# Moving GpSimd's wait on the transposes two gathers earlier in a deformable convolution with a following 3x3 convolution

## The reference

```python
x = x + _L0_conv_ref(_gn(x), w_offset, b_offset, w_conv, b_conv, gamma, beta)
x = x + _L1_conv_ref(_gn(x), weight, bias)
```

## Time and profile before

| | |
|---|---|
| median of 3 runs | 948.3 us (947.69 to 948.37) |
| profiled execution, own time | 948.03 us |
| its span, first to last instruction | 946.3 us |
| mean granted TensorE clock | 0.805 |
| gathers, first and last start | 16.1 and 828.6 us |

### The profile page before, as it was taken

One profiled execution on the slowest core, in us unless ns is written; L12 is line 12 of the kernel. 1 busy time (PEld: TensorE's weight loads), 2 busy tenths in 40 slices (PEclk: granted clock), 3 DMA queues, 4 the chain that ended last, 5 costly groups with the idle time before them and its releaser, 6 DMA issues.

```text
span 946.3 us, 8953 instructions
## 1 busy us (share of the span) xinstructions
PE 748.1 (79%) x2436; PEld 351.1 (37%) x2436; DVE 795.8 (84%) x1533; ACT 375.0 (40%) x1026; POOL 669.2 (71%) x731
## 2 busy tenths in 40 slices
PE   7688778877877877787778788778678776879998
PEld 5342322322322322232223323223222222667776
DVE  3789989888889989888899899888889889866664
ACT  3433435434333435433434345343343344453210
POOL 3777777777777777777777777777777777737551
PEclk9876778878768778976887878787797785599999
DMA  7777777777777777777777777777777777711111
GB/s 274 233 200 209 211 210 210 210 209 212 209 211 211 209 212 209 212 209 210 210 210 210 210 212 210 210 212 209 211 209 211 209 210 211 210 33 51 51 51 50
DMA packets 56246, 181.39 MB, mean 192 GB/s; under 512 B 11012, under 2 KB 12036, under 8 KB 55812
## 3 DMA queue, kind: packets, MB, share of 16 engines
q0 software_dynamic: 51840, 169.91, 62.5%
q1 hardware_dynamic: 3924, 10.32, 2.9%
q10 hardware_dynamic: 432, 0.59, 0.2%
HBM read 176.06 MB, written 4.72 MB: 191 GB/s over the span
## 4 chain that ended last, share of the span: by engine, by line
POOL 36%; PE 18%; DVE 18%; issue 14%; DMA 12%; ACT 1%; DVEq 0%; POOLq 0%; ACTq 0%
POOL g L388 36%; DMA g<-corner_table,idx 12%; DVE g L952 7%; PE TP L593 2%; PE PA L593 2%; PE CO L593 2%; PE CO L495 2%; PE TP L507 2%; DVE PA L965 2%; DVE PA L968 2%; DVE acc L971 2%; PE OMT L443 2%; PE VU L593 1%; PE OMT L593 1%; PE PA L438 1%
## 5 line engine op out<-in xcount | busy, mean ns | idle before, releaser
L388 POOL DMA_INDIRECT g<-corner_table,idx x648 | 613.3, 947 | 212.9 <-issue 180.7
L682 ACT ACTIVATE PA<-g,wt 128x128 f32<-128x128 f32 x642 | 203.4, 358 | 459.1 <-DMA g<-corner_table,idx 256.1
L952 DVE TENSOR_TENSOR g<-g,PA 128x1152 f32<-128x1152 f32 (+1 forms) x217 | 291.4, 1343 | 51.5 <-DMA g<-corner_table,idx 50.9
L495 PE MATMUL CO<-cols,wcs 128*128 128x384 f32 (+1 forms) x504 | 260.2, 619 | 78.7 <-ACT cols L663 77.5
L507 PE MATMUL TP<-ident,acc 128*128 128x128 f32 x648 | 146.9, 347 | 101.3 <-DVE acc L971 98.7
L443 PE MATMUL OMT<-xn,woff 128*27 128x384 f32 (+2 forms) x450 | 187.3, 534 | 3.2 <-DVE wt L878 2.0
L495 PEld LDWEIGHTS CO<-cols,wcs 128*128 128x128 f32 x504 | 92.8, 238 | 223.5 <-ACT cols L663 193.7
L507 PEld LDWEIGHTS TP<-ident,acc 128*128 128x128 f32 x648 | 89.1, 171 | 224.9 <-DVE acc L971 211.3
L965 DVE TENSOR_TENSOR PA<-g,PA 128x384 f32<-128x384 f32 x214 | 120.6, 564 | 19.1 <-ACT PA L682 1.2
L968 DVE TENSOR_TENSOR PA<-g,PA 128x384 f32<-128x384 f32 x214 | 119.8, 560 | 5.9
L971 DVE TENSOR_TENSOR acc<-g,PA 128x384 f32<-128x384 f32 x214 | 118.0, 552 | 5.9
(11 more groups left out here) (148 smaller groups left out, 525.9 us busy)
## 6 DMA issues: line engine op xcount, KB each, us to landing
g<-corner_table,idx POOLq DMA_INDIRECT x648, 3.7
out_dram<-x SPq DMA_DIRECT2D x16, 288.0 KB, 2.1
x<-x_dram SPq DMA_DIRECT2D x3, 1152.0 KB, 7.8
x<-x_dram ACTq DMA_DIRECT2D x3, 192.0 KB, 4.2
x<-x_dram SPq DMA_DIRECT2D x3, 192.0 KB, 3.9
wconv<-wconv_dram SPq DMA_DIRECT2D x1, 576.0 KB, 5.0
w<-w_dram SPq DMA_DIRECT2D x1, 576.0 KB, 10.0
grid<-grid_dram SPq DMA_DIRECT2D x1, 162.0 KB, 4.2
```

The costliest lines, as they stand in the source:

```text
L388: pl.indirect_dma_start(out=g[:, k, t].rearrange("p q c -> p (q c)"), out_offset=None, in_=tab_d, in_offset=bass.IndirectOffsetOnAxis(ap=i ...
L495: last = nc.tensor.matmul(co_bank(c, t)[:, t * P:t * P + size], wcs[:, c // CHUNKS % 2, k, :], cols[:, s % TURNS, n * P:n * P + size], sta ...
L682: last = nc.scalar.activation(first[:, n] if s < LAST_SUMS else g[:, k, t, 0, :], g[:, k, t, 0, :], ACT.Copy, scale=wt0[:, c % 2, t, k:k + 1])
L952: nc.vector.tensor_tensor(corners[:, :, 1:4, :], corners[:, :, 1:4, :], weights[:, :, 1:4].unsqueeze(3).to_broadcast([P, size, 3, P]), ALU ...
```

## The change

The wait on `turned` stands inside the loop over an item's gathers: ahead of the second gather of item s (of the only one where an item has one), and it asks that item s + 1 - 4, that is s - 3, is turned. That is the same semaphore value which the kernel before asks for ahead of the first gather of item s + 1, two gathers later. The first gather of an item has no wait on `turned` of its own any more.

```diff
-                    if first_item(c) + i >= LEAD:
-
-                        pl.wait_ge(turned, first_item(c) + i - LEAD + 1)
-                    for k, t in units:
+                    s = first_item(c) + i
+                    for n, (k, t) in enumerate(units):
+                        if n == min(1, len(units) - 1) and s + 1 >= LEAD:
+
+                            pl.wait_ge(turned, s + 1 - LEAD + 1)
                         pl.indirect_dma_start(
```

## The result

Eight runs of the changed kernel have a median of 954.4 us (951.7 to 955.9), eight of the kernel before 948.1 us (945.8 to 949.8). The ratio is 1.0065 with a 95% interval of 1.0050 to 1.0079: slower by 6.2 us (4.7 to 7.5). The forecast was 955.2 us, 6.9 us slower. The profiled execution after has a span of 952.7 us, 6.4 us more than before.

A forecast was written before the change was run, and what follows sets the result against it. The prediction took POOL's gather pace, 1.25 us each with no stall made up, as the bound. Its terms 1.5 + 1.70 + 1.94 + 0.66 + 0.79 + 0.29 = 6.88 us gave 955.2 us, range 951.5 to 960.

The forecast's parts named there:

- POOL's own pace sets the end: From 16 to 829 us gathers start every 1.25 us; no interval makes up for an earlier stall, so delays move the end.
- the first rival: Stalls are absorbed: DVE, the busiest engine, sets the pace and POOL catches up; 948.3 us, chance 5%.
- The price is the lateness of the turns: Cost is how late item s - 3's transposes, plus 0.27 us release, come for item s's second gather; 6.88 us summed.
- The third rival: A release in mid-item is dearer: 0.5 us more at each of seven places, 3.5 in all; 958.7 us, chance 14%.
- start, to item 9: Chunk 0: item 4's second gather waits for item 1 until 36.74, part comes back at 52.98; bounds 1.26 and 2.1, taken 1.5 us.
- chunk 2 (items 18, 19): After the second image's group norm statistics: item 18's gather 0.58 us late, item 19's needs 93.43 against 91.73; 1.70 us in all.
- chunk 8 (item 72): After 2.85 us of DVE statistics at 285.35, item 72's gather at 290.56 needs 292.50: 1.94 us.
- chunk 14 (items 126, 127): Third place after group norm statistics: item 126's gather at 493.21 must wait until 493.87, 0.66 us.
- items 141 to 145: Where DVE computes a group norm's scale; the largest delay is item 145, 564.49 against 565.28: 0.79 us.
- item 177: Its second gather at 684.58 must wait until 684.87: 0.29 us.
- end, item 216: Its wait of 0.58 us costs nothing: the gather lands at 832.81, before DVE reaches the item at 833.83.
- the second rival: Turns come sooner, since part of the lateness is PE's own queue: 4.4 us in all, 952.7 us, chance 18%.

The follow-up runs named there:

- the faster kernel: Kernel before, but the first-gather wait asks for item s - 5 only and, at chunk changes, each gather waits for its own buffer's sum: 0.9976, -2.3 us.
- the control: Kernel before with five of six group norm statistics instructions left out for images 2 to 4: 1.0004 (0.9994 to 1.0014).
- all but the start: Changed kernel with the old wait up to item 8 and the moved wait from item 9 on: 1.0039, +3.7 us against the kernel before.
- before, less statistics: Kernel before with only the first of six group norm statistics instructions kept for images 2 to 4: 1.0004 (0.9994 to 1.0014).
- start alone: Changed kernel with the moved wait for items 3 to 8 only and the old wait from item 9 on: 1.0017, +1.6 us against the kernel before.
- after, less statistics: Changed kernel with five of six group norm statistics instructions left out for images 2 to 4: 1.0019, +1.8 us against the kernel before.
- the other direction: Kernel before with the first-gather wait asking for item s - 5, and per-buffer waits on sums at chunk changes: 0.9976, median 945.8 us.

## Why the prediction was right

**POOL's own pace sets the end.** Shown from three sides: stalls are never made up (no interval between gathers in the changed kernel is under 1.24 us), removing 2.2 us of stalls (2.98 us over the usual idle time before, 0.75 in the faster kernel) gains 2.3 us, and removing 7 us of DVE's work gains nothing. From item 9's third gather to item 215's first, 616 intervals, all six traces whose later waits are no sooner than before take 770.5 to 770.7 us, the one with less work on DVE among them. Nor is this pace that of a backlog of transfers: behind the stall at 31.19 in the changed kernel, where the DMA engines' share from 30 to 32 us was 0.14, the next gather again came 1.25 us later, at 32.44.

Removing DVE's work is the direct test of the first rival. By the Trainium skill (Perfetto Trace Analysis, Identifying the Most-Contended Engine) the engine of highest occupancy is the most contended one and is to be optimized first; that would be DVE, with 84% against POOL's 71%. The trace and the control disagree. What the occupancy leaves out is the idle time of 0.30 us before nearly every one of the 648 gathers, which no wait explains.

**The price is the lateness of the turns.** Shown by the dose: with the same value asked for one, two, three and six gathers sooner the loss is 1.6, 6.2, 29.9 and 370 us, and at the new place with the old value nothing. The third rival, a dearer release, fell: the 15 gathers that the changed kernel's trace holds back start 0.27 us after the transposes, as was taken. The 0.77 us at 52.98, on which it rested, go with the place. In the trace of six gathers sooner the first gather of every chunk but chunk 0 starts 0.77 to 0.80 us after the transposes, and nearly all others 0.27. Ahead of a chunk's first gather other waits stand too; whether they are the reason was not tried.

**The terms.** The sum was 6.88 us and the trace has 6.4. Its parts were less well sized, so that the sum came this close is partly luck. The parts are read as the shift of the gathers across each place, from the profiled execution before to the one after:

| place | forecast | measured |
|---|---|---|
| start, to item 9 | 1.5 | 1.8 |
| chunk 2 (items 18, 19) | 1.70 | 0.75 |
| chunk 8 (item 72) | 1.94 | 0.32 |
| chunk 14 (items 126, 127) | 0.66 | 1.83 |
| items 141 to 145 | 0.79 | 0 |
| item 177 | 0.29 | 0.08 |
| items 37, 87, 117, 132, 133 | 0 | 1.2 |
| end, item 216 | 0 | 0.5 |

Most of these can be read. For chunk 14, items 141 to 145 and the end the size turned on TensorE's granted clock, which the prediction did not look at. In the traces it is at one of two levels, 0.50 and 1.00 of full speed (1.2 and 2.4 GHz). Four matmuls of an offset convolution take 2.76 us at the lower one and 1.47 at the upper, the two of a contraction 1.65 and 0.91, and the transposes behind them come that much later. At which places the lower level falls differs from one execution to the next.

The start shows it. In the kernel before, PE stands idle for 4.39 us ahead of item 0's transposes, and they find the clock at the lower level. When it is back differs between executions. PE in the same stretch of the kernel before and of the control with less statistics, whose chunk 0 is the same (window, its length, PE's busy time and instructions, granted clock, DMA share, GB/s):

```profile
32.00:34.00 2.00, 2.00 (x5) 0.50 0.67 195
```

```profile
32.00:34.00 2.00, 2.00 (x8) 0.84 0.70 184
```

The table sets the start of six traces side by side:

| run | wait in chunk 0 | mean granted clock, 28 to 40 us | first gather to item 9's first, us |
|---|---|---|---|
| all but the start | old | 0.57 | 38.0 |
| before | old | 0.72 | 36.9 |
| before, less statistics | old | 0.86 | 34.6 |
| after | moved | 0.72 | 38.8 |
| start alone | moved | 0.86 | 36.4 |
| after, less statistics | moved | 0.86 | 36.1 |

At the same clock the moved wait costs 1.9 us (at 0.72) or 1.5 to 1.8 (at 0.86), as forecast. But with the old wait the start alone differs by 3.4 us between executions, in step with the clock, more than the change costs there. In the control item 1 is turned 1.5 us sooner than before, and the wait of 2.04 us at item 5 is gone.

Chunk 8's term held a late landing: that of the last gather of item 68, just ahead of the statistics. In the trace of the kernel before, that gather and DVE's start on the item:

```profile
276.79 0.96 POOL L388 DMA_INDIRECT g<-corner_table,idx  x1 [0.30 <-issue]
...
282.23 1.35 DVE L952 TENSOR_TENSOR g<-g,PA 128x1152 f32<-128x1152 f32 x1 [1.63 <-DMA g<-corner_table,idx]
```

It is 5.44 us. After, the same pair, then the statistics and item 72's gather behind item 69's transposes:

```profile
279.60 0.95 POOL L389 DMA_INDIRECT g<-corner_table,idx  x1 [0.30 <-issue]
...
283.41 1.35 DVE L953 TENSOR_TENSOR g<-g,PA 128x1152 f32<-128x1152 f32 x1
...
286.52 2.85 DVE L835 BATCH_NORM_STATS2 bst<-x 128x6 f32<-128x384 f32 x6
...
292.84 0.55 PE L508 MATMUL TP<-ident,acc 128*128 128x128 f32 x3 [1.35 <-DVE acc L972]
293.66 0.94 POOL L389 DMA_INDIRECT g<-corner_table,idx  x1 [0.62 <-PE TP L508]
```

3.81 us, 1.63 less: just what is missing from the term of 1.94. The late landing is no accident of one execution. Six of eight traces compared have it (last section), and the profiled execution after is one of the two without. In the run with all but the start changed it is there (5.2 us), and item 72 waits 1.66.

Chunk 14 went the other way, through PE's queue at the lower clock. Items 126 and 127 after, with what PE does between the transposes of items 123 and 124:

```profile
496.30 0.90 PE L508 MATMUL TP<-ident,acc 128*128 128x128 f32 x3 [1.35 <-DVE acc L972]
...
497.13 2.76 PE L444 MATMUL OMT<-xn,woff 128*27 128x384 f32 x4
497.48 0.94 POOL L389 DMA_INDIRECT g<-corner_table,idx  x1 [0.90 <-PE TP L508]
...
498.81 0.55 DVE L972 TENSOR_TENSOR acc<-g,PA 128x384 f32<-128x384 f32 x1
...
499.82 1.65 PE L496 MATMUL CO<-cols,wcs 128*128 128x384 f32 x2
...
501.26 0.85 PE L508 MATMUL TP<-ident,acc 128*128 128x128 f32 x3
...
502.39 0.94 POOL L389 DMA_INDIRECT g<-corner_table,idx  x1 [1.47 <-PE TP L508]
```

Item 124 was summed at 499.36, but turned only at 502.11, behind an offset convolution of 2.76 us and a contraction of 1.65 us; the same pairs of instructions take 1.47 and 0.91 us just ahead, at 490.60 and 492.00. The granted clock was 0.50 from 496 to 502 us; in the kernel before it was 1.00 over these six us, and item 124 was turned 1.50 us after its sum instead of 2.75. PE in a part of this stretch, before and after:

```profile
498.00:500.00 2.00, 2.00 (x9) 1.00 0.67 221
```

```profile
498.00:500.00 2.00, 2.00 (x4) 0.50 0.55 174
```

At items 141 to 145 it is the reverse. Before, item 142 was turned behind an offset convolution of 2.76 us (at 560.87), after behind one of 1.47 (565.83), and the term of 0.79 fell to nothing. So part of a turn's lateness is PE's, as the second rival said, but it falls on either side.

The last is the end. Item 216's wait was to cost nothing, covered by DVE. The chain that ended last after has it:

```profile
834.67 1.28 PE OMT L439 x6
835.95 0.65 PE TP L508 x3
836.61 0.26 issue
836.87 3.40 DMA g<-corner_table,idx
840.26 0.02 issue
840.29 0.57 DVE g L953
```

The transposes of item 213 stood behind a contraction and PE's warm-up matmuls (line 439, whose result is not used), at a granted clock of 0.50 from 824 to 836 us, and ended at 836.60 instead of the expected 828.89 + 5.95 = 834.84. Before, the clock was 1.00 when they ran, from 828 us on. The wait became 2.3 us, more than the cover of 1.6 us (833.83 less the landing at 828.58 + 3.65), and 0.5 us came through.

So the mechanism was right, and the sum was right with some luck. The terms were read from one execution and hold where a late landing and the lower clock fell in it; the places that had little room in it were left at zero. Four terms were too large, by 3.6 us together, and the others too small by 3.2, which nearly cancelled.

## What to carry to other kernels

Before asking which engine is busiest, divide the time between the first and last start of a repeated instruction by its count. An engine that issues at a constant interval, also right behind a stall, may be the limit at a lower occupancy than another; here each stall on it was lost for good. A wait that is moved ahead costs the lateness of its releaser at the few places with a backlog, so price it place by place. Where DVE or PE has extra work take the size from more than one execution, and compare only stretches with the same granted clock. And where two stalls stand close together, easing the first alone may gain nothing, since it hands its time to the second (+0.4 us here, -0.7 to 1.4); removing the second alone gained 1.4 us, and easing both 2.3.

## What was not expected of the hardware

Some gathers land late at nearly the same items in kernels whose gathers are differently timed: the last gathers of items 68, 84, 113, 144, 158 and 189 reach DVE 4.3 to 5.8 us after their start in at least six of the eight kernels compared (before, after, one gather sooner, old value at the new place, start alone, all but the start, less statistics, the other direction), against a median landing of 3.7. What delays them wasn't tried and stays open.

TensorE's mean granted clock was lower where PE stood idle more: 0.805 of full speed before, with PE busy 79% of the span, and 0.688 in the kernel that waits for item s - 2, with PE busy 66%; the same 2436 matmuls were busy 867.9 us there instead of 748.1.
